# A pass's gathers issued one by one: each waits on GpSimd until the preceding gather has landed

## What is computed

```python
x = x + 0.5 * _L0_ffn_ref(_layernorm(x), ...)      # layer 0, and again as layer 2
x = x + _L0_attn_ref(_layernorm(x), ...)           # layer 1, RWKV
x = x + 0.5 * _L1_ffn_ref(_layernorm(x), ...)      # layer 3, and again as layer 5
x = x + _L1_attn_ref(_layernorm(x), ...)           # layer 4, retention
# in a mixture: top-2 of 8 experts for each token, softmax weights over the two,
# h = silu(x @ Wg[e]) * (x @ Wu[e])  (or silu(x @ we1[e] + be1[e])),  y = h @ Wd[e]
```

## Time and profile before

| | us |
|---|---|
| runs: 818.47, 818.75, 823.67; median | 818.75 |
| the profiled execution, its own time | 820.56 |
| its span, on which all rows stand | 818.7 |
| PE busy | 633.4 |
| DVE / ACT / POOL busy | 387.9 / 342.5 / 387.3 |
| mean granted TensorE clock | 0.886 |

### The profile page before, as it was taken

The page is one execution under the profiler, slowest core; times in us unless marked ns, Lnnn a source line. Parts: engine busy times, 40 slices in busy tenths (PEclk is TensorE's granted clock), DMA queues, the critical chain, the costliest instruction groups (busy, mean ns, idle before and its releaser), DMA issues.

```text
span 818.7 us, 12941 instructions
## 1 busy us (share of the span) xinstructions
PE 633.4 (77%) x4180; PEld 540.2 (66%) x4180; DVE 387.9 (47%) x1056; ACT 342.5 (42%) x667; POOL 387.3 (47%) x400
## 2 busy tenths in 40 slices
PE   2478977997489786887867875899967999966782
PEld 2377767787467785876766875766743558856772
DVE  6442115696549661514240304079688785410202
ACT  2334545654266343343445542632321324633451
POOL 1544755454544345536355354572212285456532
PEclk9998997999699898769889887999977999979887
DMA  9641122012301113112032013110030011212203
GB/s 339 198 145 34 36 71 56 27 33 62 81 27 29 23 56 91 36 49 45 28 97 65 28 36 84 38 37 8 20 87 8 21 37 33 59 39 85 61 27 113
DMA packets 45119, 50.19 MB, mean 61 GB/s; under 512 B 14456, under 2 KB 36344, under 8 KB 45056
## 3 DMA queue, kind: packets, MB, share of 16 engines
q0 software_dynamic: 11776, 24.14, 12.3%
q1 hardware_dynamic: 33280, 25.23, 9.7%
HBM read 32.04 MB, written 17.29 MB: 60 GB/s over the span
## 4 chain that ended last, share of the span: by engine, by line
PE 48%; another core or an unknown queue 10%; DVE 8%; issue 5%; ACT 4%; DMA 2%; POOL 1%; ACTq 1%; DVEq 0%; SPq 0%; POOLq 0%
PE bank L612 13%; PE bank L599 9%; PE bank L592 8%; PE pair L700 4%; PE pair L732 3%; PE bank L573 2%; PE pair L526 1%; DVE hT L1252 1%; PE pair L536 1%; ACT w_up L831 1%; DMA xs<-tokens_in,idx_in 1%; ACT hT L852 1%; PE pair L516 1%; PE bank L615 1%
## 5 line engine op out<-in xcount | busy, mean ns | idle before, releaser
L1086 POOL DMA_INDIRECT tokens_out<-ys,idx_out x184 | 189.5, 1030 | 241.4 <-ACT ys L899 194.2
L1076 POOL DMA_INDIRECT xs<-tokens_in,idx_in x184 | 188.1, 1022 | 167.3 <-PE bank L573 59.2
L612 PE MATMUL bank<-w,hT 128*128 x1288 | 191.8, 296 | 52.2 <-ACT hT L852 20.3
L612 PEld LDWEIGHTS bank<-w,hT 128*128 128x128 f32 x1288 | 175.3, 208 | 69.5 <-issue 68.6
L592 PE MATMUL bank<-xT_kept,w_up 128*128 128x128 f32 x1104 | 173.9, 307 | 47.1 <-ACT gate L849 13.2
L592 PEld LDWEIGHTS bank<-xT_kept,w_up 128*128 128x128 f32 x1104 | 157.9, 218 | 65.8 <-issue 34.7
L831 ACT ACTIVATE w_up<-w 128x728 f32 (+1 forms) x184 | 129.3, 718 | 47.1 <-DVE owner L1232 19.0
L1252 DVE TENSOR_TENSOR hT<-gate,bank 128x384 f32<-128x384 f32 x92 | 50.7, 552 | 177.0 <-PE bank L592 75.3
L599 PE MATMUL bank<-xT_kept,w_up 128*128 128x128 f32 x736 | 107.3, 296 | 17.7 <-ACT hT L852 8.1
L599 PEld LDWEIGHTS bank<-xT_kept,w_up 128*128 128x128 f32 x736 | 98.1, 207 | 26.4 <-issue 17.8
L852 ACT ACTIVATE hT<-bank 128x512 f32<-128x512 f32 x92 | 54.6, 595 | 109.9 <-PE bank L599 50.6
(11 more groups left out here) (169 smaller groups left out, 626.0 us busy)
## 6 DMA issues: line engine op xcount, KB each, us to landing
yg<-tokens_out SPq DMA_DIRECT2D x64, 128.0 KB
w<-in_w SPq DMA_DIRECT2D x8, 536.0 KB, 8.4
w<-in_w SPq DMA_DIRECT2D x8, 512.0 KB
xs<-tokens_in,idx_in POOLq DMA_INDIRECT x184
tokens_out<-ys,idx_out POOLq DMA_INDIRECT x184
tokens_in<-xn SPq DMA_DIRECT2D x8, 256.0 KB
tokens_in<-xn SPq DMA_DIRECT2D x8, 254.0 KB
out<-x SPq DMA_DIRECT2D x8, 128.0 KB
```

The lines of the kernel that those rows point to most:

```text
L612: last = mm(y, hT[0:n_f, n % 2, c * P:(c + 1) * P], w_of(k, e, WD[k] + c * P, P, n_f), start=(c == 0), stop=(k == 0 and c == CH[k] - 1))
L1076: pool.indirect_dma_start(xs[:, j % RING, :], None, xn_dram[KIND[f]][b], tile_rows(idx_in, b, j))\
L1086: pool.indirect_dma_start(ys_dram[b], tile_rows(idx_out, b, j), ys[:, j % RING, :], None)\
```

## The change

Inside `gather`, before every gather except a pass's first, GpSimd also waits until the preceding gather of the same pass has landed. Nothing else differs: the order of the streams, the rings, the number of DMAs and their sizes are the same. 22 waits for each of the 8 passes are added, 176 in all. Scatters get no wait.

```diff
                     if p or j >= RING:
                         before = (p, j - RING) if j >= RING else (p - 1, max(i for i in range(TILES) if i % RING == j))
                         pool.wait_ge(xT_ready, before[0] * NGR + GROUP_OF[before[1]] + 1)
+                    if j:
+                        pool.wait_ge(ld_xs[(j - 1) % RING], 16 * (ring_uses(p, j - 1) + 1))
                     pool.indirect_dma_start(xs[:, j % RING, :], None, xn_dram[KIND[f]][b], tile_rows(idx_in, b, j))\
                         .then_inc(ld_xs[j % RING], 16)
```

## The result

| | before | changed |
|---|---|---|
| median of 5 runs (us) | 818.75 | 971.58 |
| lowest, highest | 818.47, 823.67 | 970.59, 976.76 |
| the profiled execution, its span | 820.56, 818.7 | 976.76, 974.8 |
| PE busy | 633.4 | 683.5 |
| POOL busy | 387.3 | 387.2 |

The ratio is 1.187 (95% interval 1.182 to 1.191). The forecast was 820 with a range of 793 to 845, so the change is slower by far more than any of the cases allowed.

A forecast was written before the change was run, and what follows sets the result against it. The prediction took no engine as full, with about 82 us of waits for PE increments held during back-to-back indirect DMAs. Late gathers +25 us and releases -24 us sum to +1, giving 820 us, range 793 to 845.

The forecast's parts named there:

- What bounds the kernel: No engine full; PE's increments held during back-to-back indirect DMAs, released after the run drains; about 82 us of waits.
- The price of a bound wait: Between neighbouring gathers on POOL: 2.5 us in place of 1.26, 1.25 more; bounds 2.3 and 4.1.
- POOL is busy for under half the span, so most of this falls into its idle time: Up to 146 us more on POOL from 117 neighbours, mostly hidden because tiles are needed only every 3 to 4 us.
- In the other passes the sum of the extra never reaches a transpose: Outside passes 0, 2, 6 and 7 first gathers go out long before they are needed, so no cost.
- Pass 0: Gathers beside six weight loads land in 5 us, making T4 late by 10 us; bounds 3 and 20.
- Passes 2, 6 and 7: Late gathers ahead of transposes T4, T3 and T6 cost 2, 9 and 4 us.
- Cost and gain: Late gathers cost 25 us, between 11 and 38; timely PE increments give back 24 us; sum +1 us.
- C: Late gathers win, in pass 0 beside the weight loads and T3 of pass 6: 844 us; chance 0.32.
- The prediction's B: Releases of held increments win, in passes 1, 3, 4 and 5: 794 us; chance 0.33.
- D: Nothing happens, as POOL is idle half the time: 819 us; counted with the forecast, together 0.35.
- The chain's share of the unknown pieces: Sign: "another core or an unknown queue" falls from 10% to about 5% of the chain.
- no piece of over 5 us lies in a run of gathers alone: Sign in the chain's unknown-queue share: no such piece over 5 us; this failing means late gathers win.

The follow-up runs named there:

- e10: Kernel before the change, every indirect DMA, scatters too, held back until the preceding one has landed: 1344.15 us; repeated on a chip with late increments: 1347.74 us.
- e2: Changed kernel, each gather waiting for the gather two before it instead of the preceding one: 801.39 us beside 804.94 for the kernel before (0.997).
- e8: Kernel before, wait for the preceding gather only at tiles 4, 8, 12, 16, 20: 714.75 us beside 677.13 on one chip, 811.94 beside 803.61 on another.
- e1b: Changed kernel with its two waits exchanged, the landing's now on the DMA instruction itself: 885.2 us beside 677.13 for the kernel before (1.308).
- e6: Changed kernel, new wait kept only at the 117 gathers right behind a gather of their pass: 920.97 us beside 678.5 for the kernel before (1.354).
- e4_no_reg: Kernel before without TensorE's register loads, always expert 0's weights, so values aren't the reference's: 680.59 us beside 678.5 for the kernel before (1.000).
- c4: Changed kernel as it is, run again on a chip without late increments: 954.53 us beside 677.13 for the kernel before (1.408).
- c2_before: Kernel before as it is, profiled on a chip with late increments: 805.92 us.
- e5: Kernel before, all 23 owners of a pass loaded into 23 registers at its first down product: 840.86 us beside 816.22 for the kernel before (1.035).

## Why the prediction was wrong, point by point

**What bounds the kernel: right, for its chip.** Increments of PE come out late in bursts of indirect DMAs; with no two in flight they don't (e10). That they come out once the burst has drained, as the prediction inferred, e2 and e8 do not bear out. That this is not so on every chip could not be read from one trace.

**The price of a bound wait: mis-sized.** The prediction took 2.42 for the landing and 0.18 for the wake, and 2.5 us from gather to gather. Counted as the earlier trace rows count, up to the semaphore's last step, a neighbour's landing takes 2.67 us in the changed kernel (median), a quarter of a microsecond more than was taken. The wake was taken from a start after a DVE instruction, 0.18 us. Measured it is 0.74, or 0.26 with the wait on the DMA itself (e1b); counted from the last data packet it is 1.08 and 0.6. So the distance is 3.3 to 3.4 us, and the extra 2.0 to 2.1 and not 1.25. The bound of 4.1 held this value; the middle should have gone towards it, since no row showed a start released by a landing.

**"POOL is busy for under half the span, so most of this falls into its idle time": the step that failed.** All the waits were to cost 25 us, of up to 146 that the neighbours add to GpSimd by the prediction; on a quiet chip they cost 242.5 us, as much as the 117 x 2.1 = 246 that they really add, and 165 of it shows as idle time of PE (e6). A second sum beside the first would have shown it: where gathers are neighbours a tile needs a gather and, later, a scatter, 3.3 + 1.28 = 4.6 us of POOL's stream, against the 3 to 4 us at which the prediction itself had PE use tiles. With the prediction's own 2.5 us it is 3.8, already at the upper end. And the idle time was, by the rows, of the wrong kind; this part is argued and no run tests it. 194.2 us of it, the largest single part, was scatters waiting for the y copy, which is downstream of the very gathers that come late; delaying a gather delays the copy too, and that idle time would move along instead of being used up. It did fall to 92.4 on a holding chip. On quiet ones it was 105.4 without the waits (e4_no_reg) and 77.0 with them (c4), so little of it was used up there.

**"In the other passes the sum of the extra never reaches a transpose": wrong.** At 3.3 to 3.4 us the twelve gathers of pass 2's opening take 283.91 - 246.64 = 37.3 us instead of the 27.5 forecast, T4's last tile is 39.7 us after the first gather instead of 29.9, and the 75 waits of transposes are spread over all eight passes.

**Pass 0: right on the loads, too small in all.** The three gathers beside the weight loads landed in 5.50, 4.74 and 3.98 us (to the last packet); 5 was taken. The prediction says that the trace before has no landing beside them. Its timelines show none, but its DMA packets have six, of 5.9 to 6.5 us. T4 was put at 62.1, 10 late; it begins at 65.08 and its last tile at 68.03, some 16 late, since each gather after the loads takes 3.3 us and not 2.5:

```profile
65.08 0.49 PE L573 MATMUL bank<-const,xs 128*128 128x128 f32 x3
68.03 0.33 PE L573 MATMUL bank<-const,xs 128*128 128x128 f32 x1 [2.46 <-DMA xs<-tokens_in,idx_in]
```

**Passes 2, 6 and 7: too small.** T3 of pass 6 was put 21.9 us after the pass's first gather (the prediction's own terms, 3.96 + 17.5, make 21.5); its last tile comes 759.31 - 729.16 = 30.2 after it. In pass 7 the last tile of T6 comes 73.3 us after the first gather, where it came 54.3 after it before: 19 later, and 4 were forecast.

**Cost and gain.** Cost 25 forecast, 277 measured where nothing else changes (c4). Gain 24 forecast, 101 to 125 as the difference of the two kinds of chip, with the open reading named there. The prediction brought 82 us of waits down to 32 pass by pass, and took another quarter off because PE is busy 77% of the span; but much of PE's idle time was there *because* of the late increments, and on a quiet chip the nearest kernel (e4_no_reg) has PE busy for 86%. Both terms were off, the cost eleven-fold, and that they were of one size in the forecast rested on two discounts that did not hold.

**The rivals.** C had the right sign and mechanism (late gathers). But its places were too few, and 844 was far too low, since C used the same 2.5 us and the same idle time. Its rule is that the fixed setup of a DMA overlaps if it is issued early and waited on late (the Trainium skill, DMA: Bandwidth & Descriptors, "Rules for kernel authors", which says it of a DMA beside compute). The trace agrees for gathers beside gathers: neighbours stand at 3.3 instead of 1.26 us. The prediction's B, the releases, is a real effect, but no run has it alone. D, nothing happens, is ruled out by the result.

**The signs that were named.** The chain's share of the unknown pieces fell to 1%, not 5%, and no piece of over 5 us lies in a run of gathers alone, so by that sign the prediction's B or the forecast should have come true. "Neighbours 2.4 to 2.6 us apart" failed at once, with 3.3, and was the sign that mattered.

## What to carry to other kernels

Before sinking an added wait into an engine's idle time, ask what that idle time waits for: if it is downstream of the delayed work, it may move along and hide little. Sum the engine's stream per tile in the densest stretch, and take the wake of a wait from a start that was released by the same kind of event, or from the far bound where no row has one. And when a limit on overlap seems needed, try two in flight first: on a holding chip that cost nothing here, where one in flight cost 153 to 176 us. And measure a limit where nothing else keeps the engines waiting: e8's 40 waits cost 8.3 us on a holding chip and 37.6 on a quiet one.

## What the runs showed of the hardware that was not expected

- The same program takes 677 to 679 us on two chips and 804 to 819 on the others. On the slower ones TensorE increments come out late while indirect DMAs overlap (138.3 us of waits in c2_before), and on the faster ones no trace has such a wait; with one indirect DMA in flight at a time the kinds are 0.3% apart.
- A gather that waits for a landing starts 0.26 us after the last step of its semaphore (0.6 after the last data packet) if the DMA instruction carries the wait, and 0.74 us (1.08) after it if a second wait makes it an instruction of its own. The order of two `wait_ge` in the code decided which, and was worth 69.3 of 954.5 us.
- A register load of TensorE costs nothing measurable between products (1.000 without the 184 loads on a quiet chip), but 23 in a row kept a product waiting for 7.76 us (e5).
